# Where the first loads are issued: chunk 0 wholly on SP's queue, chunk 2 behind ScalarE's table load

## The chip, the cores and the metric

The kernel runs on one core of a Trainium2 chip. Times are microseconds (us) on the device; the profile measures one execution, and the runs are further executions. The engines are TensorE (PE, with its weight loads as PEld), VectorE (DVE), ScalarE (ACT), GpSimd (POOL) and SyncE (SP), which only issues transfers here. A queue is where an engine's transfers are issued: q1 in the profile carries those that SP issues, q10 those of ScalarE. Both are served by the core's 16 DMA engines.

## What is computed

The input x has 32 x 64 = 2048 tokens of 1024 values, all in float32.

```python
base   = einsum('btd,od->bto', x, W)                     # 1024 x 1024
logits = einsum('btd,ed->bte', x, Wr) + 5.0 * one_hot(language_ids)   # 8 experts
topw, topi = top_k(logits, 2)
gates  = sum(one_hot(topi) * softmax(topw))
h      = einsum('btd,erd->bter', x, A)                   # rank 16 for each expert
y      = base + 2.0 * einsum('bter,bte,eor->bto', h, gates, B)
out    = x + einsum('bti,oi->bto', y, (U * S) @ V.T)     # rank 256
```

## The kernel before

The last step has rank 256, so the kernel never forms y. It first makes the product of V and W, a 1024 x 256 matrix (in the code `proj`), and that of B and V (`bv`). Then it goes over 16 tiles of 128 tokens: x times `proj` (together with the columns of A and Wr), the gates, the gated rank part times `bv`, a transposition, and the product with U times S, to which x is added.

float32 products are made of float32r ones. Each operand is split into a `hi` part, a cast made by ScalarE, and a `lo` part, the rest, made by VectorE (GpSimd for x). Three multiplications (hi hi, hi lo, lo hi; the helper `triple`, lines 244 to 246) give one product. So each piece of V and W goes load, ScalarE (`v_hi` line 417, `w_hi` line 413), VectorE (`v_lo` line 492, `w_lo` line 487), TensorE.

The first phase runs over 16 chunks: V and W are cut into 8 chunks of 128 rows, and W into a left and a right half of 512 columns. Chunk k, from 0 to 7, holds 256 columns of V and the left half of W in one array `VW`, 384 KB, and has a semaphore `vw_load[k]`. The right halves (`w_raw`) come as chunks 8 to 15. TensorE makes 12 multiplications for each chunk, in order. Chunk 0 is loaded in two pieces of 192 KB: V with the first 128 columns of W, and the other 384 columns, with a semaphore `vw_rest_load`; its 12 multiplications stand in `p_first` (lines 259, 264, 269), those of the other chunks in `p_chunk`. While the first load is under way TensorE multiplies zeros (line 374).

Each engine's program is written out by hand and runs in its written order; semaphores join them. SP issues chunk 0's first piece, then chunks 1 and 3 to 7, then ids, the right halves, A, B, U and x. ScalarE issues chunk 0's second piece and chunk 2, then runs one Exp of a single column (`act_warm`), in front of which the compiled program has the load of its function table, and then the casts. The Exp reads `iota_e`, which GpSimd writes, and waits for that (`const`). After the first phase come the 16 tiles (`step`), and the stores at the end.

Of the kernel before, what the change touches and what calls it, by code (L numbers as in the profile page):

```python
# [16 lines left out]
def adaln_ffn(nc, xt, x, ids, VW, W, AW, B, U, S, out):  # L17
    P = 128
    TILES, _, DC, _ = xt.shape
    D = DC * P  # L20
    E = 8
    ER = AW.shape[2] - E
    R = ER // E
    OC, _, HQ = W.shape
    O = OC * P
    RANK = U.shape[1] * P
# [18 lines left out]
    with ExitStack() as ctx:  # L45
        def sb(name, shape, dt):
            return ctx.enter_context(nc.sbuf_tensor(name, shape, dt))
# [4 lines left out]
        def sem(name):  # L52
            return ctx.enter_context(nc.semaphore(name))
# [5 lines left out]
        vw_raw = sb("vw_raw", [P, OC, RANK + HQ], F32)  # L59
# [46 lines left out]
        vw_load = [sem(f"vw_load{k}") for k in range(OC)]  # L106
        vw_rest_load = sem("vw_rest_load")
# [52 lines left out]
        def w_chunk(i):  # L160
            return vw_raw[:, i, RANK:RANK + HQ] if i < OC else w_raw[:, i - OC, :]
# [4 lines left out]
        @block.sync  # L166
        def _(sp):
            def load_w(k):
                sp.dma_start(w_raw[:, k, :], W[k, :, :]).then_inc(w_load[k], 16)

            def load_xt(t):
                if t >= XTR:
                    sp.wait_ge(xt_lo, t - XTR + 1)
                sp.dma_start(xt_raw[:, t % XTR, :, :], xt[t, :, :, :]).then_inc(xt_load[t % XTR], 16)

            def load_x(t):
                if t >= XR:
                    sp.wait_ge(stored[t % XR], 16 * (t // XR))
                sp.dma_start(x_all[:, t % XR, :], x_v[t, :, :]).then_inc(x_load[t % XR], 16)

            def store(t):
                sp.wait_ge(fin_free, HALF * t + HALF)
                sp.dma_start(out_v[t, :, :], x_all[:, t % XR, :]).then_inc(stored[t % XR], 16)

            first = RANK + P
            sp.dma_start(vw_raw[:, 0, 0:first], VW[0, :, 0:first]).then_inc(vw_load[0], 16)
            for k in (1, *range(3, OC)):
                sp.dma_start(vw_raw[:, k, :], VW[k, :, :]).then_inc(vw_load[k], 16)
            sp.dma_start(ids_i[:, :], ids).then_inc(ids_load, 16)
            load_w(0)  # L190
            load_w(1)
            sp.dma_start(aw_raw[:, :, :], AW).then_inc(aw_load, 16)
            load_xt(0)
            load_w(2)
            load_w(3)
            sp.dma_start(b_raw[:, :, :], B).then_inc(b_load, 16)
            for k in range(4, OC):
                load_w(k)
            load_xt(1)
            sp.dma_start(s_col[:, :], S).then_inc(s_load, 16)  # L200
            sp.dma_start(u_raw[:, :, :], U).then_inc(u_load, 16)
            for t in range(2, XTR):
                load_xt(t)
            for t in range(XR):
                load_x(t)
            for s in range(TILES):
                if s + XTR < TILES:
                    load_xt(s + XTR)
                if s >= 3 and s - 3 + XR < TILES:
                    load_x(s - 3 + XR)  # L210
                if s >= 2:
                    store(s - 2)
            for n in range(HALF):
                cols = slice(n * BANK, (n + 1) * BANK)
                sp.wait_ge(fin_free, HALF * (LAST - 1) + n + 1)
                sp.dma_start(out_v[LAST - 1, :, cols], x_all[:, (LAST - 1) % XR, cols]).then_inc(stored[(LAST - 1) % XR], 16)
            for n in range(3):
                lo, hi = ((0, BANK), (BANK, BANK + BANK // 2), (BANK + BANK // 2, D))[n]
                sp.wait_ge(fin_free, HALF * LAST + n + 1)
                sp.dma_start(out_v[LAST, :, lo:hi], x_all[:, LAST % XR, lo:hi]).then_inc(stored[LAST % XR], 16)  # L220
            for j in range(XR):
                n = len(range(j, TILES, XR)) + (2 if j == LAST % XR else 1 if j == (LAST - 1) % XR else 0)
                sp.wait_ge(stored[j], 16 * n)
# [176 lines left out]
        @block.scalar  # L400
        def _(act):
            def split_w(i):
                h, k = divmod(i, OC)
                if i == 0:
                    nc.scalar.copy(w_hi[:, 0, 0:P], w_chunk(0)[:, 0:P]).then_inc(w_hi_done, 1)
                    act.wait_ge(vw_rest_load, 16)
                    nc.scalar.copy(w_hi[:, 0, P:HQ], w_chunk(0)[:, P:HQ]).then_inc(w_hi_done, 1)
                    return
                if i >= OC:
                    act.wait_ge(w_load[i - OC], 16)  # L410
                if i >= WRING:
                    act.wait_ge(w_used, i - WRING + 1)
                nc.scalar.copy(w_hi[:, i % WRING, :], w_chunk(i)).then_inc(w_hi_done, 1)

            def split_v(k):
                act.wait_ge(vw_load[k], 16)
                nc.scalar.copy(v_hi[:, k, :], vw_raw[:, k, 0:RANK]).then_inc(v_hi_done, 1)

            def split_p(b):
                act.wait_ge(w_used, OC if b < 2 else 2 * OC)  # L420
                nc.scalar.copy(proj_hi[:, 2 * b:2 * b + 2, Z0:COLS],
                               fin[b][:, :].rearrange("p (c n) -> p c n", c=2)).then_inc(p_hi, 1)

            def split_x(t):
                act.wait_ge(xt_load[t % XTR], 16 * (t // XTR + 1))
                if t >= 2:
                    act.wait_ge(pj_done, t - 1)
                nc.scalar.copy(xT_hi[:, t % 2, :, :], xt_raw[:, t % XTR, :, :]).then_inc(xt_hi, 1)  # L428

            def scale_u(m):  # L430
                nc.scalar.activation(us_hi[:, m, :], u_raw[:, m, :], ACT.Copy,  # L431
                                     scale=s_col[:, m:m + 1]).then_inc(us_hi_done, 1)

            def step(s):
                if s >= 1 and s + 1 < TILES:
                    split_x(s + 1)
                if s >= 1:
                    act.wait_ge(gt_done, s)
                    nc.scalar.copy(ghT_hi[:, :], gt[:, 0:P]).then_inc(gt_hi, 1)  # L439
                    act.wait_ge(z_done, s)  # L440
                    nc.scalar.copy(z_sb[:, :], pj[(s - 1) % 2][:, Z0:COLS]).then_inc(z_copied, 1)  # L441
                    act.wait_ge(zt_done, s)
                    nc.scalar.copy(zT_hi[:, (s - 1) % 2, :], zt[:, 0:RANK]).then_inc(zt_hi, 1)  # L443
                if s < TILES:
                    act.wait_ge(dtop_ready, s + 1)
                    nc.scalar.activation(etop[:, :], dtop[:, :], ACT.Exp, accum_out=esum[:, :]).then_inc(exp_done, 1)

            first = RANK + P
            act.dma_start(vw_raw[:, 0, first:], VW[0, :, first:]).then_inc(vw_rest_load, 16)
            act.dma_start(vw_raw[:, 2, :], VW[2, :, :]).then_inc(vw_load[2], 16)  # L450
            act.wait_ge(const, 3 + E)
            nc.scalar.activation(esum[:, :], iota_e[:, 0:1], ACT.Exp).then_inc(act_warm, 1)
            act.wait_ge(act_warm, 1)
            for i in range(2 * OC):
                if i < OC:
                    split_v(i)
                split_w(i)
                if i == OC + 1:
                    act.wait_ge(aw_load, 16)
                    nc.scalar.copy(proj_hi[:, :, 0:Z0], aw_raw[:, :, :]).then_inc(aw_hi, 1)  # L460
                if i == OC + 3:
                    split_p(0)
                    split_p(1)
                if i == OC + 4:
                    split_x(0)
                if i == OC + 6:
                    act.wait_ge(b_load, 16)
                    nc.scalar.copy(b_hi[:, :, :], b_raw[:, :, :]).then_inc(b_hi_done, 1)
            split_p(2)
            split_p(3)  # L470
            split_x(1)
            step(0)
            act.wait_ge(s_load, 16)
            act.wait_ge(u_load, 16)
            scale_u(0)
            act.wait_ge(bv_done, 1)
            nc.scalar.activation(bv_hi[:, :], bv_ps, ACT.Copy, scale=SCALING).then_inc(bv_hi_done, 1)
            scale_u(1)
            for s in range(1, TILES + 1):
                step(s)  # L480
# [186 lines left out]
```

## Time and profile before

| | |
|---|---|
| Runs before | 162.08, 162.8, 163.09 us; median 162.8 |
| The profiled execution | 161.95 us |
| Span of its profile | 160.2 us |
| TensorE busy | 154.1 us, 96% of the span |
| VectorE, ScalarE, GpSimd busy | 81.6, 55.5, 40.4 us |
| Moved by DMA | 32.69 MB, 204 GB/s over the span |

The span is that of the instructions which the profile shows; the execution's own time is 1.75 us longer. A TensorE that is busy 96% of the time is one that the others keep fed nearly everywhere.

### The profile page before, as it was taken

Reading aid. Unit: us, or ns where it says so; the run is one execution under the profiler, and the core shown is the slowest. Engines: PE = TensorE matmul, PEld = TensorE weight load, DVE = VectorE, ACT = ScalarE, POOL = GpSimd, SP = SyncE. Lnnn points to the kernel's source line nnn. Section 1 sums busy time; section 2 is a strip of 40 time slices with the busy share of each in tenths; the row PEclk is TensorE's granted clock in tenths of the full one; section 3 lists DMA queues with packets and bytes.
Section 4 is the critical chain, followed back from the end, with each engine's and each line's share of the span. In section 5 each row is a group of like instructions: output and inputs, shape, how many; then the busy total and the mean of one; then the engine's idle time right before and its main releaser. Section 6 shows DMA issues by size and latency. Waiting matters only on the chain.

```text
span 160.2 us, 2469 instructions
## 1 busy us (share of the span) xinstructions
PE 154.1 (96%) x900; PEld 142.4 (89%) x900; DVE 81.6 (51%) x260; ACT 55.5 (35%) x132; POOL 40.4 (25%) x31
## 2 busy tenths in 40 slices
PE   7599999999999999999999999999999999999992
PEld 4499999998998999999998989898989898989882
DVE  0696983455946263535444453536262717081843
ACT  4684881526334323241404041414141414111210
POOL 2000060072354150606060505142323323200000
PEclk9999999999999999999999999999999999999999
DMA  5999999973300859283837474656553430303055
GB/s 176 391 403 406 392 410 408 409 302 125 128 7 0 260 208 314 100 301 119 278 131 262 141 252 158 241 169 224 197 200 131 131 131 0 131 4 131 0 202 191
DMA packets 10522, 32.69 MB, mean 204 GB/s; under 512 B 1424, under 2 KB 1936, under 8 KB 10384
## 3 DMA queue, kind: packets, MB, share of 16 engines
q1 hardware_dynamic: 10224, 31.96, 54.5%
q10 hardware_dynamic: 288, 0.59, 1.0%
q8 instruction: 7, 0.11, 0.3%
q14 instruction: 3, 0.02, 0.1%
HBM read 24.16 MB, written 8.39 MB: 203 GB/s over the span
## 4 chain that ended last, share of the span: by engine, by line
PE 91%; DMA 3%; ACT 2%; DVE 1%; issue 0%; SPq 0%
PE pj L244 15%; PE pj L246 15%; PE pj L245 15%; PE fin L244 14%; PE fin L246 14%; PE fin L245 14%; DMA vw_raw<-in_VW 3%; PE zt L303 2%; PE gt L291 1%; ACT us_hi L431 1%; PE zt L246 1%; PE zt L244 1%; PE zt L245 1%; ACT xT_hi L428 1%; DVE w_lo L487 0%
## 5 line engine op out<-in xcount | busy, mean ns | idle before, releaser
L237 POOL TENSOR_TENSOR xT_lo<-xt_raw,xT_hi 128x1024 fp32r<-128x1024 f32 x16 | 39.3, 2454 | 95.8 <-ACT xT_hi L428 95.8
L244 PE MATMUL pj<-proj_hi,xT_hi 128*128 128x392 f32 x128 | 45.1, 352 | 0.0
L246 PE MATMUL pj<-proj_hi,xT_lo 128*128 128x392 f32 x128 | 43.6, 341 | 0.0
L245 PE MATMUL pj<-proj_lo,xT_hi 128*128 128x392 f32 x128 | 43.4, 339 | 0.0
L244 PE MATMUL fin<-us_hi,zT_hi 128*128 128x512 f32 (+1 forms) x66 | 27.0, 409 | 0.0
L246 PE MATMUL fin<-us_hi,zT_lo 128*128 128x512 f32 (+1 forms) x66 | 25.6, 388 | 0.0
L245 PE MATMUL fin<-us_lo,zT_hi 128*128 128x512 f32 (+1 forms) x66 | 25.6, 388 | 0.0
L244 PEld LDWEIGHTS pj<-proj_hi,xT_hi 128*128 128x128 f32 x128 | 24.0, 188 | 1.2
L245 PEld LDWEIGHTS pj<-proj_lo,xT_hi 128*128 128x128 f32 x128 | 24.1, 188 | 0.6
L246 PEld LDWEIGHTS pj<-proj_hi,xT_lo 128*128 128x128 f32 x128 | 24.0, 188 | 0.0
L520 DVE SCALAR_TENSOR_TENSOR logit<-target,pj 128x8 f32<-128x8 f32 x16 | 2.6, 163 | 40.6 <-PE pj L246 40.6
L565 DVE TENSOR_TENSOR x_all<-fin,x_all 128x512 f32<-128x512 f32 x31 | 21.2, 686 | 2.5 <-PE fin L246 2.5
L244 PE MATMUL fin<-v_hi,w_hi 128*128 128x256 f32 x60 | 17.1, 285 | 1.4 <-DVE w_lo L487 1.4
L245 PE MATMUL fin<-v_lo,w_hi 128*128 128x256 f32 x60 | 17.0, 283 | 0.0
L246 PE MATMUL fin<-v_hi,w_lo 128*128 128x256 f32 x60 | 17.0, 283 | 0.0
L428 ACT CAST xT_hi<-xt_raw 128x1024 fp32r<-128x1024 f32 x16 | 16.6, 1040 | 0.0
L441 ACT COPY z_sb<-pj 128x256 f32<-128x256 f32 x16 | 6.0, 374 | 25.8 <-PE pj L246 25.8
L246 PEld LDWEIGHTS fin<-us_hi,zT_lo 128*128 128x128 f32 x66 | 12.4, 188 | 2.8
L439 ACT CAST ghT_hi<-gt 128x128 fp32r<-128x128 f32 x16 | 4.3, 266 | 30.3 <-PE gt L291 30.3
L244 PEld LDWEIGHTS fin<-us_hi,zT_hi 128*128 128x128 f32 x66 | 12.4, 188 | 2.1
L245 PEld LDWEIGHTS fin<-us_lo,zT_hi 128*128 128x128 f32 x66 | 12.5, 189 | 2.0
L443 ACT CAST zT_hi<-zt 128x256 fp32r<-128x256 f32 x16 | 6.0, 374 | 22.2 <-PE zt L303 22.2
(71 smaller groups left out, 188.8 us busy)
## 6 DMA issues: line engine op xcount, KB each, us to landing
xt_raw<-in_xt SPq DMA_DIRECT2D x16, 512.0 KB, 4.1
x_all<-in_x SPq DMA_DIRECT2D x16, 512.0 KB, 3.6
out<-x_all SPq DMA_DIRECT2D x14, 512.0 KB, 2.9
vw_raw<-in_VW SPq DMA_DIRECT2D x6, 384.0 KB, 6.1
w_raw<-in_W SPq DMA_DIRECT2D x8, 256.0 KB, 9.8
u_raw<-in_U SPq DMA_DIRECT2D x1, 1024.0 KB, 13.0
out<-x_all SPq DMA_DIRECT2D x3, 256.0 KB, 2.0
aw_raw<-in_AW SPq DMA_DIRECT2D x1, 544.0 KB, 8.1
```

The costliest lines, as they stand in the source:

```text
L237: nc.gpsimd.tensor_sub(xT_lo[:, t % 2, :, :], xt_raw[:, t % XTR, :, :], xT_hi[:, t % 2, :, :].bitcast(F32)).then_inc(xt_lo, 1)
L244: nc.tensor.matmul(dst, l_hi, r_hi, start=first, stop=False, skip_group_check=shared)
L245: nc.tensor.matmul(dst, l_hi, r_lo, start=False, stop=False, skip_group_check=shared)
L246: return nc.tensor.matmul(dst, l_lo, r_hi, start=False, stop=last, skip_group_check=shared)
L291: nc.tensor.transpose(gt[:, 0:P], gh[:, :], ident[:, :]).then_inc(gt_done, 1)
L303: last = nc.tensor.transpose(zt[:, m * P:(m + 1) * P], z_sb[:, m * P:(m + 1) * P], ident[:, :])
L428: nc.scalar.copy(xT_hi[:, t % 2, :, :], xt_raw[:, t % XTR, :, :]).then_inc(xt_hi, 1)
L439: nc.scalar.copy(ghT_hi[:, :], gt[:, 0:P]).then_inc(gt_hi, 1)
L441: nc.scalar.copy(z_sb[:, :], pj[(s - 1) % 2][:, Z0:COLS]).then_inc(z_copied, 1)
L443: nc.scalar.copy(zT_hi[:, (s - 1) % 2, :], zt[:, 0:RANK]).then_inc(zt_hi, 1)
L520: nc.vector.scalar_tensor_tensor(logit[:, :], target[:, s, :], LANG_BIAS, pj[q][:, LOG:LOG + E], ALU.mult, ALU.add).then_inc(gate_step, 1)
L565: nc.vector.tensor_add(x_all[:, t % XR, cols], fin_bank(i)[:, :], x_all[:, t % XR, cols]).then_inc(fin_free, 1)
```

## The change

Chunk 0's second piece is issued by SP, between the first piece and chunk 1. ScalarE issues chunk 2 behind its Exp instead of ahead of it. Nothing else is altered; from there on line numbers differ by one or two.

```diff
             sp.dma_start(vw_raw[:, 0, 0:first], VW[0, :, 0:first]).then_inc(vw_load[0], 16)
+            sp.dma_start(vw_raw[:, 0, first:], VW[0, :, first:]).then_inc(vw_rest_load, 16)
             for k in (1, *range(3, OC)):
                 sp.dma_start(vw_raw[:, k, :], VW[k, :, :]).then_inc(vw_load[k], 16)
...
-            first = RANK + P
-            act.dma_start(vw_raw[:, 0, first:], VW[0, :, first:]).then_inc(vw_rest_load, 16)
-            act.dma_start(vw_raw[:, 2, :], VW[2, :, :]).then_inc(vw_load[2], 16)
             act.wait_ge(const, 3 + E)
             nc.scalar.activation(esum[:, :], iota_e[:, 0:1], ACT.Exp).then_inc(act_warm, 1)
+            act.dma_start(vw_raw[:, 2, :], VW[2, :, :]).then_inc(vw_load[2], 16)
             act.wait_ge(act_warm, 1)
```

ScalarE's program at its start, before. Each row is an instruction with what it writes and reads, and the semaphores that it waits for.

```order
L449 DMA vw_raw<-in_VW 128x384
L450 DMA vw_raw<-in_VW 128x768
L452 ACT_TABLE_LOAD
L452 ACTIVATE esum<-iota_e 128x1 [waits const]
L417 CAST v_hi<-vw_raw 128x256 [waits vw_load0,act_warm]
L405 CAST w_hi<-vw_raw 128x128
L407 CAST w_hi<-vw_raw 128x384 [waits vw_rest_load]
L417 CAST v_hi<-vw_raw 128x256 [waits vw_load1]
```

And ScalarE's program at its start after the change:

```order
L450 ACT_TABLE_LOAD
L450 ACTIVATE esum<-iota_e 128x1 [waits const]
L451 DMA vw_raw<-in_VW 128x768
L418 CAST v_hi<-vw_raw 128x256 [waits vw_load0,act_warm]
L406 CAST w_hi<-vw_raw 128x128
L408 CAST w_hi<-vw_raw 128x384 [waits vw_rest_load]
L418 CAST v_hi<-vw_raw 128x256 [waits vw_load1]
```

The piece of 384 columns is gone from it, and the chunk of 768 columns, chunk 2, stands behind the table load and the Exp.

SP's first instructions after the change; before, the second of these rows was not there:

```order
L186 DMA vw_raw<-in_VW 128x384
L187 DMA vw_raw<-in_VW 128x384
L189 DMA vw_raw<-in_VW 128x768 x6
L190 DMA ids_i<-in_ids 128x16
L169 DMA w_raw<-in_W 128x512 x2
```

Every load that SP issues from chunk 1 on stands one place further back.

## Rows read from the trace of the kernel before

**Rows 1.** Stretch, its us, busy us of PE, PEld, DVE, ACT, POOL; clock, DMA share, GB/s.
```profile
0.00:7.74 7.74, 4.83 (x19) 3.39 (x19) 2.29 (x5) 4.21 (x10) 1.12 (x15) 1.00 0.78 280
7.74:29.43 21.69, 21.69 (x181) 21.69 (x182) 15.47 (x25) 12.82 (x24) 2.41 (x1) 1.00 1.04 404
29.43:47.00 17.57, 17.33 (x109) 16.91 (x108) 11.62 (x31) 8.14 (x16) 7.86 (x3) 1.00 0.50 188
47.00:157.00 110.00, 110.00 (x596) 100.40 (x595) 51.82 (x200) 30.30 (x84) 29.00 (x13) 1.00 0.46 163
```

**Rows 2.** Waits of TensorE, then of ScalarE, from 0 to 30 us.
```profile
PE fin L244 <- DVE w_lo L487: 1.4, 1, 1.4
...
ACT v_hi L417 <- DMA vw_raw<-in_VW: 1.9, 2, 1.3
```

**Rows 3.** The chain that ended last, in order of time (start, us, what).
```profile
0.74 0.38 SPq L186
1.17 4.84 DMA vw_raw<-in_VW
6.03 0.41 ACT v_hi L417
6.44 0.53 ACT w_hi L413
6.99 0.70 DVE w_lo L487
7.74 0.39 PE fin L244
```

**Rows 4.** Timeline from 0 to 8 us: start, us, engine, line, operation.
```profile
0.73 0.40 ACTq L449 DMA_DIRECT2D vw_raw<-in_VW  x1
...
1.16 0.46 ACTq L450 DMA_DIRECT2D vw_raw<-in_VW  x1
1.17 2.85 SPq L188 DMA_DIRECT2D vw_raw<-in_VW  x6
...
1.55 0.33 POOL L234 MEMSET iota_e<- 128x1 f32 x8
1.65 1.28 ACT L452 ACT_TABLE_LOAD   x1 [1.65 <-PEq L657]
2.94 0.20 ACT L452 ACTIVATE esum<-iota_e 128x1 f32<-128x1 f32 x1
3.69 0.41 ACT L417 CAST v_hi<-vw_raw 128x256 fp32r<-128x256 f32 x1 [0.54 <-DMA vw_raw<-in_VW]
...
5.70 0.64 PE L269 MATMUL fin<-v_hi,w_lo 128*128 128x256 f32 x4
...
6.87 0.40 ACT L417 CAST v_hi<-vw_raw 128x256 fp32r<-128x256 f32 x1
```

**Rows 5.** DMA queues from 1 to 2.05 us: packets, MB, share of 16 engines.
```profile
q1 hardware_dynamic: 28, 0.04, 19.7%
```

**Rows 6.** DMA queues from 2.05 to 2.1 us.
```profile
q10 hardware_dynamic: 1, 0.00, 8.1%
```

**Rows 7.** DMA queues from 1 to 3.43 us.
```profile
q1 hardware_dynamic: 174, 0.29, 43.8%
q10 hardware_dynamic: 144, 0.20, 21.9%
```

**Rows 8.** DMA queues from 3.43 to 5.7 us.
```profile
DMA packets 307, 0.85 MB, mean 374 GB/s; under 512 B 31, under 2 KB 31, under 8 KB 307
q1 hardware_dynamic: 164, 0.45, 56.9%
q10 hardware_dynamic: 143, 0.39, 45.3%
```

**Rows 9.** The issue of chunk 2 on ScalarE, line 450, and its landing.
```profile
L450 ACTq DMA_DIRECT2D vw_raw<-in_VW x1: 461/461/461, 1.2 to 1.2; - x1
...
DMA to landing us min/median/max: 5.0/5.0/5.0
```

## The prediction

> **What bounds the kernel now.** The first view read is the busy time of each engine in four stretches [rows 1]. From 7.74 us on TensorE hardly pauses: it is busy 21.69 of 21.69 us, then 17.33 of 17.57 us, then all of 110.00 us, and the granted clock is 1.00 in every row. Only in the first 7.74 us is there room: 4.83 us busy. What is left behind 157 us is the last addition and the stores, which the edit does not touch. So the edit, which concerns the first microseconds alone, can move the end by as much as it moves the point at which the unbroken run of TensorE begins, and by nothing else.
>
> The second view is the list of waits [rows 2]. TensorE's one real wait there is 1.4 us at line 244, the first multiplication of chunk 1, released by VectorE's w_lo. ScalarE has two waits for a load, 1.9 us together. The third view, the chain in order of time, says what stands behind both [rows 3]: the load of chunk 1 is issued at 1.17 and lands 4.84 us later, at 6.01. ScalarE casts V from 6.03 and W up to 6.97, VectorE makes w_lo from 6.99 to 7.69, and TensorE begins chunk 1 at 7.74. From landing to TensorE it is 7.74 - 6.01 = 1.73 us, and none of that is edited.
>
> Chunk 0, whose second piece the edit moves, is not the bound. The timeline shows its last four multiplications starting at 5.70 and running 0.64 us [rows 4], so TensorE is through with it at 6.34 and idle for 1.40 us. The table load (1.65 to 2.93) and the warming Exp (to 3.14) are not the bound either: the cast that follows them starts at 3.69, at the landing of chunk 0's first piece. **Everything turns on one number, the landing of chunk 1.**
>
> **What that landing depends on.** The two queues' traffic in stretches of time tells it. Up to 2.05 us only SP's queue, q1, has moved anything [rows 5]. ScalarE's queue, q10, has its first packet in the next 0.05 us [rows 6]: 2.05 - 0.73 = 1.32 us after its first issue. By 3.43 us [rows 7] q10 has moved 0.20 MB, which is its piece of chunk 0 (192 KB, 0.197 MB) and nothing of chunk 2. q1 has moved 0.29 MB, its own 0.197 MB piece and some 0.09 MB of chunk 1. From 3.43 to 5.70 us [rows 8] q10 moves 0.39 MB, just chunk 2, while q1 moves 0.45 MB: the 0.30 MB that chunk 1 (0.393 MB) still lacked, and a part of chunk 3. The total is 374 GB/s, of which q1 gets 0.45 / 2.27 = 198 GB/s. So chunk 1 shares the DMA engines with chunk 2 for its last 0.30 MB. At that rate it would be through at 3.43 + 1.52 = 4.95; it lands at 6.01. The 1.06 us between are the slowest of 16 engines and the completion, which I take as unchanged.
>
> **Part 1, chunk 0's second piece goes to SP's queue.** The bytes that have to move ahead of chunk 1's end are the same as before: all of chunk 0, as SP's piece and the other piece ran side by side. Now the two run one behind the other, then chunk 1. At equal total rate q1 alone has moved the same 0.49 MB at 3.43 us [rows 7], and chunk 1 still lacks 0.30 MB. Cost of the bytes: 0. The issue itself takes 0.43 us on SP (its neighbours, six issues in 2.85 us, take 0.475 each with their gaps [rows 4]); it pushes chunk 1's issue from 1.17 to 1.60 and every later issue of SP by as much. q1's first packet came at 1.75 or later (no more than 0.04 MB by 2.05), about 1.0 us after its issue at 0.74, so chunk 1 is ready to move at about 2.6. By then q1 has not emptied chunk 0's 0.39 MB, which at the total rate takes until about 3.1. The 0.43 us is hidden behind those bytes; uncovered it would cost all of 0.43. The later loads of SP sit in a queue that is full anyway: 404 GB/s was moved by all engines up to 29 us, and ScalarE waits for no load there but the two named. Taken: 0.
>
> **Part 2, chunk 2's load goes behind the table load.** ScalarE's stream now starts with the table load, at about 0.73, where its first issue began. It takes 1.28 us and ends near 2.01, the last iota write is done at 1.88, and the Exp takes 0.20, to about 2.2 [rows 4]. ScalarE's issue of chunk 2 then starts between 2.02 (beside the Exp) and 2.25, and takes some 0.46 us as before [rows 9]. With 1.32 us from issue to first packet, chunk 2 starts to move between 3.34 and 3.57. Before, it started at 3.43, behind its queue mate. **The two halves of the edit nearly cancel:** chunk 2 used to be held back by a load ahead of it in the queue, and is now held back by the table load, for nearly the same time.
>
> The price of the difference: for each microsecond that chunk 2 starts later, q1 moves 374 - 198 = 176 KB more, which at 198 GB/s brings chunk 1 forward by 0.89 us. Starting at 3.34 costs 0.09 x 0.89 = 0.08 us; starting at 3.57 gains 0.14 x 0.89 = 0.12 us. I take the upper end, an issue behind the Exp, since in the trace ScalarE's issues and the table load follow one another without overlap (1.16 + 0.46 = 1.62, then 1.65): a gain of 0.1 us. Chunk 2 landed at 1.16 + 5.0 = 6.16 us [rows 9] and would at 6.3, and ScalarE reaches it at 6.87 before [rows 4], so it stays hidden. The 0.46 us of issuing on ScalarE ends by 2.7, ahead of chunk 0's cast at 3.69 or a little sooner. Chunk 0 itself may come a few tenths earlier, into the 1.40 us in which TensorE waits for chunk 1: worth nothing.
>
> **The sum.** Chunk 1 begins on TensorE at 7.74 - 0.1 = 7.64. The profiled execution took 161.95 us for a span of 160.2 us, and would take 161.85. The runs before have a median of 162.8, 0.85 above the profiled one, and lie 1.0 us apart. The same 0.1 off the median gives 162.7 us.
>
> **Rival A, chunk 1 gets the DMA engines to itself.** If chunk 2's first packet comes at or after chunk 1's last, chunk 1's missing 0.30 MB moves at 374 instead of 198 GB/s: 0.80 instead of 1.52 us, a gain of 0.7. TensorE would start chunk 1 at 7.0, still behind chunk 0's end at 6.34, so all of it counts: 162.8 - 0.7 = 162.1. It wants chunk 2's issue at 4.23 - 1.32 = 2.9 or later, 0.65 later than I have it. For it speaks that nothing in the trace shows an issue behind an Exp, and that a queue's packets may start later than the one case of 1.32; against it that the Exp took up its work 0.01 us after the table load. The Trainium skill, page "ScalarE: Activation LUTs", section "What ACT_TABLE_LOAD costs", prices a switch of tables at 1.28 us of load and about 1.38 us of drain; an estimate by it puts the issue near 3.6 and is this rival in full. By that page the time would be 162.1, while rows 4 show the load's 1.28 and no drain behind it. Chance 0.18.
>
> **Rival B, the late issue decides, and the kernel is slower.** If q1 takes up chunk 1 a fixed time after its issue and not when the ring ahead of it is empty, chunk 1 lands at 1.60 + 4.84 = 6.44 and TensorE starts it 0.43 later: 162.8 + 0.43 = 163.2. It decides from the point where chunk 1 is ready later than q1 has emptied chunk 0, 2.6 against 3.1 by my figures; the full price needs another 0.43 beyond that, or a queue that loses as much rate by running alone. For it speaks that q1 alone moved only 0.04 MB up to 2.05 us [rows 5], which the start of the engines may or may not explain, and that no row has one queue alone at the full rate before 5.7 us; against it that chunk 1's bytes followed chunk 0's on q1 before 3.43 us [rows 7] with no gap that the total shows. The Trainium skill, page "DMA: Bandwidth & Descriptors", section "Issuing engines are not separate DMA queues", speaks against the change in this way: issuing from several engines saves issue time and nothing else, and this edit gives up just that. Rows 8 agree with its other half, that the queues interleave on the same engines. Chance 0.12.
>
> **Rival C, chunk 2 comes too late.** TensorE wants chunk 2 after chunk 1's 12 multiplications (15 chunks in 21.69 us [rows 1], 1.45 each), at 9.19; with 1.73 us of casting ahead it must land by 7.46, 1.3 us later than its 6.16. That takes an issue at about 3.5. From there every microsecond of delay costs one, less the 0.7 of rival A. Only a ScalarE queue held up for over 2 us would do it. Chance 0.04, about 163.3.
>
> **How the numbers follow.** The forecast, chunk 1 within 0.2 us of its old landing, has chance 0.66 and the time 162.7. Rival A 0.18 at 162.1, rival B 0.12 at 163.2, rival C 0.04. The ends of the range are A's 162.1 less 0.3 and B's 163.2 plus 0.1, for the spread of 1.0 us between the runs themselves: 161.8 to 163.3. A measurement of this kernel can hardly tell less than 1% (1.6 us) from no change, and no rival reaches that; what is left for either side is a shift of the runs. Faster by over 1% 0.03, within 1% 0.94, slower 0.03.
>
> **What would show it.** In the changed kernel's timeline the table load starts near 0.75 and ScalarE's issue near 2.2. q10's first packet comes near 3.5, and TensorE's wait at line 245, formerly 244, grows by what chunk 0 ends sooner; chunk 1 begins between 7.5 and 7.8. Rival A shows as a start near 7.0, rival B as one near 8.1 with q1 idle before chunk 1's packets, rival C as a second gap in TensorE behind chunk 1. The forecast is wrong if a queue's rate depends on its being alone, or if the time from issue to first packet on q10 is not 1.32 us when the issue comes later.

## The result, and the profile after

The changed kernel takes 165.52 us (median of 6 runs, 164.58 to 166.88) where the kernel before takes 162.44 (6 runs, 161.83 to 163.22). The ratio is 1.0192, with a 95% interval of 1.0132 to 1.0251: 3.1 us slower. The profiled execution took 164.58 us for a span of 162.8 us, 2.6 more than the 160.2 before.

The same stretches as [rows 1], of the changed kernel, with the first 29 us cut where its clock changes:

```profile
0.00:9.90 9.90, 6.93 (x27) 5.58 (x28) 3.46 (x8) 5.37 (x13) 1.12 (x15) 1.00 0.77 276
9.90:13.30 3.40, 3.40 (x18) 3.40 (x17) 2.86 (x7) 1.76 (x5) 0.00 (x0) 0.50 1.03 397
13.30:29.00 15.70, 15.70 (x133) 15.70 (x132) 11.55 (x16) 9.98 (x16) 2.42 (x1) 1.00 1.04 404
```

From 9.90 to 13.30 us the granted clock is 0.50, 1.2 instead of 2.4 GHz. TensorE is busy all the time but starts only 18 multiplications. The same 3.40 us of the kernel before:

```profile
9.90:13.30 3.40, 3.40 (x31) 3.40 (x30) 3.10 (x7) 2.22 (x5) 0.00 (x0) 1.00 1.04 400
```

13 fewer at 0.12 us each are 1.6 us lost. The other part of the loss stands in the chain that ended last, to be set beside [rows 3]:

```profile
0.74 0.38 SPq L186
1.17 0.42 SPq L187
1.64 5.36 DMA vw_raw<-in_VW
7.03 0.40 ACT v_hi L418
7.43 0.53 ACT w_hi L414
7.99 0.70 DVE w_lo L486
8.73 0.39 PE fin L245
```

Chunk 1 is issued at 1.64 instead of 1.17, lands 5.36 us later instead of 4.84, at 7.00 instead of 6.01, and TensorE starts it at 8.73 instead of 7.74. From landing to TensorE it is 1.73 us, as before. So the profile has 1.0 us of later start and 1.6 us of half clock, 2.6 together: all of the longer span. All six executions of the changed kernel had a mean granted clock of 0.979 to 0.99 of full speed, where one such stretch in the profile makes 0.99 and the profile of the kernel before had 1.00. The two at 0.979 are 1.7 and 2.3 us above the profiled one; 0.979 would be some 6.9 us at half clock instead of 3.4, an estimate from the mean alone. The clock is not all that differs between executions: one at 0.99 is 1.4 us above the profiled one too.

What ScalarE and SP do in the first 2.1 us (timeline, beside [rows 4]):

```profile
0.73 1.28 ACT L450 ACT_TABLE_LOAD   x1 [0.73 <-PEq L656]
...
1.64 0.42 SPq L189 DMA_DIRECT2D vw_raw<-in_VW  x1
1.93 0.37 ACTq L451 DMA_DIRECT2D vw_raw<-in_VW  x1
2.03 0.20 ACT L450 ACTIVATE esum<-iota_e 128x1 f32<-128x1 f32 x1
```

ScalarE issues chunk 2 at 1.93, within the table load and ahead of the Exp that stands in front of it in the program. The issue waited for the iota writes (1.88), not for the table.

The queues' traffic up to 3.43 us and from there to 5.7 us, as in [rows 7] and [rows 8]:

```profile
DMA packets 293, 0.41 MB, mean 168 GB/s; under 512 B 32, under 2 KB 288, under 8 KB 293
q1 hardware_dynamic: 291, 0.40, 55.5%
q10 hardware_dynamic: 2, 0.01, 2.8%
...
DMA packets 207, 0.63 MB, mean 277 GB/s; under 512 B 2, under 2 KB 2, under 8 KB 207
q1 hardware_dynamic: 106, 0.32, 46.6%
q10 hardware_dynamic: 101, 0.31, 36.4%
```

q1 has moved 0.40 MB by 3.43, chunk 0's 0.393 and hardly anything of chunk 1, where before the two queues had moved 0.49. Then the two queues together reach 277 GB/s instead of 374. Split by the microsecond, the hole stands where chunk 0's bytes end:

```profile
2.00:3.00 1.00, 1.00 (x4) 0.79 (x3) 0.00 (x0) 0.22 (x2) 0.00 (x0) 1.00 0.81 295
3.00:4.00 1.00, 0.92 (x3) 0.20 (x2) 0.28 (x1) 0.72 (x3) 0.00 (x0) 1.00 0.57 134
4.00:5.00 1.00, 0.97 (x4) 0.94 (x5) 0.82 (x2) 0.29 (x1) 0.00 (x0) 1.00 0.86 289
5.00:6.00 1.00, 1.00 (x6) 1.00 (x6) 0.02 (x1) 0.00 (x0) 0.00 (x0) 1.00 1.02 396
```

134 GB/s from 3 to 4 us, where the kernel before has 349:

```profile
3.00:4.00 1.00, 0.92 (x3) 0.20 (x1) 0.00 (x0) 0.46 (x2) 0.00 (x0) 1.00 0.98 349
```

The DMA engines had nothing to do, or waited. The question for the experiments is why.

### The profile page after: what moved, and what is told of

It reads as the page before. It is cut to its first block, busy times and chain, and to the rows that moved or that the text cites. A ratio compares the mean times of both kernels' runs of the same rounds, so it can differ in the third digit from the quotient of the medians.

```text
span 162.8 us, 2469 instructions
## 1 busy us (share of the span) xinstructions
PE 156.5 (96%) x900; PEld 144.9 (89%) x900; DVE 81.8 (50%) x260; ACT 55.6 (34%) x132; POOL 40.4 (25%) x31
## 4 chain that ended last, share of the span: by engine, by line
PE 91%; DMA 3%; ACT 2%; DVE 1%; SPq 0%; issue 0%
PE pj L245 15%; PE pj L247 15%; PE pj L246 15%; PE fin L245 14%; PE fin L247 14%; PE fin L246 14%; DMA vw_raw<-in_VW 3%; PE zt L304 2%; PE gt L292 1%; ACT us_hi L432 1%; PE zt L247 1%; PE zt L245 1%; PE zt L246 1%; ACT xT_hi L429 1%; DVE w_lo L486 0%
## 5 line engine op out<-in xcount | busy, mean ns | idle before, releaser
L245 PE MATMUL fin<-v_hi,w_hi 128*128 128x256 f32 x60 | 17.8, 297 | 1.9 <-DVE w_lo L486 1.9
L247 PE MATMUL fin<-v_hi,w_lo 128*128 128x256 f32 x60 | 17.7, 295 | 0.0
L246 PE MATMUL fin<-v_lo,w_hi 128*128 128x256 f32 x60 | 17.6, 294 | 0.0
L245 PEld LDWEIGHTS fin<-v_hi,w_hi 128*128 128x128 f32 x60 | 12.2, 204 | 2.1 <-DVE w_lo L486 2.1
```

Of the source, the lines that this page charges most:

```text
L245: nc.tensor.matmul(dst, l_hi, r_hi, start=first, stop=False, skip_group_check=shared)
L246: nc.tensor.matmul(dst, l_hi, r_lo, start=False, stop=False, skip_group_check=shared)
L247: return nc.tensor.matmul(dst, l_lo, r_hi, start=False, stop=last, skip_group_check=shared)
```

## The experiments

Times are medians. Each ratio is to runs of the kernel before on the same chip, with its 95% interval. "Lands" is issue plus time to landing, from the profile of that kernel, which is one execution. Unedited loads show how far one profile can be trusted: chunk 1 lands at 6.0 us in the kernel before, at 5.6 in e4 and at 5.4 in e14, which have the same loads, and at 7.0 in the changed kernel and 7.5 in e3, which share theirs. So the change made chunk 1 later by something between 1.0 and 2.1 us, and where the loads are shared by both queues, a difference of half a microsecond between two profiles says little. The runs are called e1 to e16; each diff is against the kernel that the text or the expectation names.

### Each half of the change alone

e1: chunk 0's second piece to SP, chunk 2 left at the head of ScalarE's program:

```diff
 sp.dma_start(vw_raw[:, 0, 0:first], ...).then_inc(vw_load[0], 16)
+sp.dma_start(vw_raw[:, 0, first:], ...).then_inc(vw_rest_load, 16)
-act.dma_start(vw_raw[:, 0, first:], ...).then_inc(vw_rest_load, 16)
```

> Only the first half of the change: chunk 0's second piece on SP's queue, chunk 2 still issued by ScalarE ahead of its table load. In the changed kernel the DMA engines moved only 134 GB/s from 3 to 4 us and chunk 1 landed at 7.0 instead of 6.0 us. Theory S (supply): chunk 1 is now the third transfer on q1, and its packets are not there when q1 has emptied chunk 0, whatever q10 does. Then chunk 1's packets on q1 again begin at 3.1 us or later for most engines, and it lands at 6.4 us or later. Rival H (the fresh queue): the gap comes from chunk 2, which as the first transfer of its queue starts at 3.2 to 4.4 us and holds the engines up. Then chunk 2 moves from 2.1 us on, there is no gap, and chunk 1 lands at 6.0 us or before. In time: S +0.5 to +1.0 us against the kernel before from the load alone, H 0. A stretch of TensorE at half clock would add up to 1.7 us.

162.99 us, ratio 1.0025 (0.9999 to 1.0052). Chunk 1, issued at 1.65, lands 4.6 us later, at 6.3. By landing this is near S. By traffic the hole of 3 to 4 us is gone (378 and 409 GB/s from 3 to 5 us), as H has it, but another one stands a microsecond earlier:

```profile
2.00:3.00 1.00, 1.00 (x4) 0.79 (x3) 0.00 (x0) 0.65 (x2) 0.00 (x0) 1.00 0.53 134
```

Here it is chunk 0 that comes late: its first piece lands 3.8 us after its issue instead of 2.9, ScalarE casts it at 4.63 instead of 3.69, and TensorE then never waits for chunk 1. Neither theory is right as it stands.

e2: chunk 2 behind the Exp, chunk 0's second piece left where it was:

```diff
-act.dma_start(vw_raw[:, 2, :], VW[2, :, :]).then_inc(vw_load[2], 16)
 act.wait_ge(const, 3 + E)
 nc.scalar.activation(esum[:, :], iota_e[:, 0:1], ACT.Exp).then_inc(act_warm, 1)
+act.dma_start(vw_raw[:, 2, :], VW[2, :, :]).then_inc(vw_load[2], 16)
```

> Only the second half of the change: chunk 2 issued by ScalarE behind table load and Exp, chunk 0's second piece still on q10 ahead of it. Theory S: chunk 1 is the second transfer on q1 as before, so it starts behind its own piece of chunk 0 and lands at 6.0 us or earlier, down to 5.3 us if chunk 2 comes late enough to leave it the engines; time 0 to -0.7 us. Rival H: chunk 2's late start holds the engines up, chunk 1 lands near 7.0 us and the time is +1.0 us or more.

163.78 us, ratio 1.0076 (1.0044 to 1.0108). Chunk 1 lands after 3.6 us, at 4.8: with less on q10 beside it, it is earlier than in any profile with the loads of before. H falls. But chunk 2, issued at 1.93, takes 6.6 us and lands at 8.56, 2.4 later than before, and the rate is 246 to 304 GB/s from 4 to 7 us. TensorE waits for it, and starts it at 10.28:

```profile
10.28 0.39 PE L244 MATMUL fin<-v_hi,w_hi 128*128 128x256 f32 x1 [0.45 <-DVE w_lo L487]
```

The kernel before starts chunk 2 at 9.19. The difference, 1.1 us, is that of the two spans (161.3 and 160.2). So the second half loses by itself, 1.1 us by the medians; the first half costs 0.3 us, at the edge of its interval. Together they cost 3.1, more than the sum of both.

### TensorE's clock

e3 and e4: the changed kernel, and the kernel before, with multiplications of zeros between chunks 0 and 1 (8 and 6 of them):

```diff
 p_first()
+for _ in range(8):
+    nc.tensor.matmul(gt[...], zeros[:, :], zero_row, start=True, stop=True)
```

> The changed kernel with 8 more multiplications of zeros (512 columns, into a bank not yet in use) between chunk 0 and chunk 1, where TensorE stood idle for 1.87 us ahead of a stretch at half clock (9.90 to 13.31 us). Theory C (clock): the idle time brings the half clock about; filled, the granted clock stays at 1.00 from the first rise to the end, and 1.7 us come back, so the time is 1.0 to 1.7 us below the changed kernel's 165.5. Rival: the clock falls by itself, and the low stretch of 3.4 us appears as before; the time is the changed kernel's or more, since the added multiplications may delay chunk 1.

164.3 us, ratio 1.0093 (1.0061 to 1.0125), 1.2 us below the changed kernel (1.6 by the two ratios). The same stretch as above:

```profile
9.90:13.30 3.40, 3.40 (x30) 3.40 (x30) 3.40 (x9) 3.08 (x8) 0.00 (x0) 1.00 1.04 402
```

No half clock, and 30 multiplications, although chunk 1 landed even later here, at 1.64 + 5.89 = 7.5. Nine of its ten executions have a mean clock of 0.998 or more; one has 0.989, at 166.2 us. Theory C holds for these nine: without the idle time ahead of chunk 1 the half clock stays away. No length of idle time at which the clock falls can be read from the runs. The kernel before idles for 1.40 us there without a fall, the changed one for 1.87 with one.

> The kernel before with 6 more multiplications of zeros between chunk 0 and chunk 1, where it idles for 1.40 us. Its profile has no stretch at half clock behind the first rise, so theory C expects no change of the profiled time beyond 0.3 us; if some of its executions do have such a stretch (they spread over 1.4 us), the median falls by up to 0.7 us and the spread narrows. Rival: the additions only delay chunk 1, +0.2 to +0.5 us.

162.71 us, ratio 1.0002 (0.9963 to 1.0041). The median says no change, but no execution lies near it: six take 161.9 to 162.1 us, six 163.3 to 164.5. For the first six C is right. The profile is one of the others, and there the rival is: the six additions start at 7.34, run at half pace until 9.4 us, and hold chunk 1 back to 9.67, though its w_lo was ready at 7.3. Half pace shows in the number of multiplications started in a microsecond, from 5 to 6 us, first in the kernel before, then in e4:

```profile
5.00:6.00 1.00, 1.00 (x10) 1.00 (x10) 0.43 (x1) 0.00 (x0) 0.00 (x0) 1.00 1.00 369
5.00:6.00 1.00, 1.00 (x6) 1.00 (x6) 0.50 (x1) 0.39 (x2) 0.00 (x0) 1.00 1.03 412
```

In e4 the multiplications of chunk 0 stand 0.21 us apart, and the full pace of 0.12 us comes at 9.4 us; in the profile of the kernel before it came before chunk 0's second four. The clock column says 1.00 in both, since it knows no level ahead of the first change. TensorE's first microseconds run at half pace, and for how long differs from one profile to the next.

e14 and e15: two kernels that take the idle time away at the start, where TensorE has nothing to do between its 6 multiplications of zeros and chunk 0:

```diff
-for n in range(6):
+for n in range(7):
     nc.tensor.matmul(fin[n % FINS][...], zeros[:, :], zero_row, start=True, stop=True)
```

This is e14; e15 has `range(8)` on top of e9's edit, below.

> The kernel before with 7 multiplications of zeros at the start instead of 6, which cover 0.43 of the 0.52 us that TensorE idles ahead of chunk 0. In the profiles TensorE comes up from half clock between 4.3 and 15.4 us, and the runs of one kernel spread over 1.5 us and more. Theory C (clock: idle time at the start delays the rise): the median falls by 0.2 to 0.8 us below 162.6 and the spread narrows. Rival: the rise does not depend on the idle time; the median stays within 0.2 us.

**161.93 us, ratio 0.9966 (0.9941 to 0.9990).** The only kernel of the sixteen that is clearly faster than the one before, by 0.55 us by the ratio, within the range that C gave. Nine of its 12 runs lie between 161.75 and 162.26; those of the kernel before beside it are spread from 161.76 to 163.44. The gain is measured. That it comes from an earlier full pace is argued: its one profile has the full pace from 6.1 us on, later than the profile of the kernel before, and its span of 159.8 also has a chunk 1 that landed at 5.4.

> All loads on SP with chunk 0 as one transfer (median 162.58, TensorE idle for 0.83 us ahead of chunk 0 and not at all ahead of chunk 1), with 8 multiplications of zeros at the start instead of 6, which last to about 4.77 us, where chunk 0 starts. TensorE then runs without a pause from 0.99 us on. Theory C: the rise comes before 7.8 us in the profile and the median falls to 161.6 to 162.3, below the kernel before. Rival: no change, 162.6 within 0.2.

162.27 us, ratio 0.9987 (0.9962 to 1.0013), with the full pace from 3.9 us on in the profile. In the expected direction and inside the range, but not apart from the kernel before.

### All on SP, or chunk 2 on SP

e5: the kernel before with chunk 2 on SP.

```diff
-for k in (1, *range(3, OC)):
+for k in range(1, OC):
     sp.dma_start(vw_raw[:, k, :], VW[k, :, :]).then_inc(vw_load[k], 16)
...
-act.dma_start(vw_raw[:, 2, :], VW[2, :, :]).then_inc(vw_load[2], 16)
```

> The kernel before with chunk 2 issued by SP between chunks 1 and 3, so that q10 carries only chunk 0's second piece, at 0.73 us. In the run with only chunk 2 moved, chunk 1 landed at 4.83 us while q10 was silent, and the slow stretch (246 to 304 GB/s from 4 to 7 us, chunk 2 landing at 8.56) came with the late issue of chunk 2. Theory L (late issue): the issue at 1.93 us on ScalarE's queue, into traffic under way, brings the slow stretch. Without it the rate stays near 400 GB/s, chunk 1 lands at 4.9 and chunk 2 at 5.9 us; TensorE has no idle time but at the start, and the time is 0.3 to 1.0 us below the kernel before. Rival T (third transfer): the third transfer on q1 is slow by itself, wherever chunk 2 is; then the stretch from 4 us on is there again, chunk 2 lands at 6.5 us or later and the time is at or above that of the kernel before.

162.60 us, ratio 0.9996 (0.9978 to 1.0014). Chunk 1 lands after 3.6 us, at 4.8, and TensorE never waits for it. The landing of chunk 1:

```profile
DMA to landing us min/median/max: 3.6/3.6/3.6
```

But the slow stretch is there without any late issue on ScalarE: chunk 2, issued at 1.6, lands at 6.9. Theory L falls as stated, T holds by the profile. The time moved by nothing; in this profile chunk 0's work at half pace lasted until 7.4 us, so that the early landing could not be used.

e6: the same edit made to the changed kernel, so that ScalarE issues nothing.

> The changed kernel with chunk 2 issued by SP between chunks 1 and 3: ScalarE issues nothing. Theory L: no slow stretch, chunk 1 lands at 4.8 to 5.1 us behind both pieces of chunk 0, chunk 2 at 5.9, time 0 to 0.8 us below the kernel before. Rival T: the third transfer on q1, chunk 1, again starts late (over 200 KB missing in 3 to 4 us as in the changed kernel) and lands near 6.5 to 7 us; time +1 to +3.

162.82 us, ratio 1.0025 (0.9997 to 1.0052). Chunk 1, issued at 1.65, lands after 4.8 us, at 6.4: T's landing, but not its time. With no late chunk 2 beside it, chunk 1 comes 0.6 us before the changed kernel's. The hole from 3 to 4 us is the same, though q10 carries nothing at all:

```profile
3.00:4.00 1.00, 0.92 (x4) 0.23 (x2) 0.32 (x1) 0.76 (x3) 0.00 (x0) 1.00 1.05 134
```

So the late chunk 2 does not make the hole. The twelve executions also price the clock within one kernel: three have a mean clock of 0.988 or 0.989 and a median of 164.3 us, the other nine have 0.997 or more and a median of 162.8.

e9: e6 with chunk 0 as one transfer.

```diff
-sp.dma_start(vw_raw[:, 0, 0:first], VW[0, :, 0:first]).then_inc(vw_load[0], 16)
-sp.dma_start(vw_raw[:, 0, first:], VW[0, :, first:]).then_inc(vw_rest_load, 16)
+sp.dma_start(vw_raw[:, 0, :], VW[0, :, :]).then_inc(vw_load[0], 16)
...
-act.wait_ge(vw_rest_load, 16)
```

> All loads on SP as in the run with all of them there, but chunk 0 as one transfer of 384 KB: chunk 1 is the second transfer on q1 and not the third, with the same bytes ahead of it. So far the third transfer on q1 landed between 6.3 and 7.7 us in every kernel, the second at 3.7 to 4.8 or, sharing with q10, at 5.6 to 6.0. Theory P (place in the queue): chunk 1 lands at 4.8 to 5.1 us, and chunk 2, now the third, at 6.3 to 7.5; TensorE has no wait ahead of chunk 1 above 0.5 us; time 162.3 to 162.8. Rival Y (bytes and moment): the rate falls near 3.3 us because q1 runs alone, and chunk 1 again lands at 6.3 us or later; time 162.8 to 165.

162.58 us, ratio 1.0003 (0.9972 to 1.0035). Chunk 1 second and issued at 1.17: it lands after 3.7 us, at 4.9. Chunk 2 is late instead, at 6.5. One issue fewer ahead of chunk 1, the same bytes, and 1.5 us gained on its landing. Y falls. One more thing differs from e6, and no run separates it: chunk 0 as one transfer goes in packets of 2 KB and more (111 of them from 1 to 3 us), as two pieces in smaller ones (254).

e10: chunk 1 instead of chunk 2 on ScalarE, at the head of its program.

```diff
-for k in (1, *range(3, OC)):
+for k in range(2, OC):
...
+act.dma_start(vw_raw[:, 1, :], VW[1, :, :]).then_inc(vw_load[1], 16)
 act.wait_ge(const, 3 + E)
```

> Both pieces of chunk 0 on SP, chunk 1 issued by ScalarE at 0.73 us ahead of the table load, chunk 2 by SP as the third transfer on q1. Theory P: chunk 1 shares the engines with chunk 0 and lands at 4.4 to 5.0 us, chunk 0 at 4.2 to 4.6, chunk 2 as the third at 6.3 to 7.0; the third's lateness is covered by TensorE's work on chunks 0 and 1, time 162.3 to 162.9. Rival Y: q10's early traffic keeps the rate up, so that chunk 2 lands at 5.9 us or before; the time is the same within the noise.

162.88 us, ratio 1.0026 (0.9997 to 1.0055). Chunk 1 lands at 4.3, chunk 2, issued at 1.6 on SP, at 7.1. P holds, a little beyond its ranges.

### Where ScalarE's issue stands

e7: the issue ahead of the Exp and its table load, but behind the wait.

```diff
 act.wait_ge(const, 3 + E)
+act.dma_start(vw_raw[:, 2, :], VW[2, :, :]).then_inc(vw_load[2], 16)
 nc.scalar.activation(esum[:, :], iota_e[:, 0:1], ACT.Exp).then_inc(act_warm, 1)
-act.dma_start(vw_raw[:, 2, :], VW[2, :, :]).then_inc(vw_load[2], 16)
```

> The changed kernel with chunk 2's issue at the same time, behind the wait for the iota writes (1.88 us), but ahead of the table load, which then runs from about 2.3 us. In the changed kernel the issue stood at 1.93, inside the table load. Theory L: the same slow stretch, chunk 1 lands at 6.5 to 7.5 us, time near the changed kernel's 165.5. Rival B (table load): the issue is slow in its effect because it runs during the table load; without that chunk 1 lands at 5.5 to 6.0 us and the time is that of the kernel before, 162.6 within 0.5.

165.64 us, ratio 1.0168 (1.0129 to 1.0206), chunk 1 at 1.64 + 6.06 = 7.7. It is not the place within the table load that makes the issue harmful: at the same moment, 1.92, it does the same harm ahead of the load. But the time is lost in another way than in the changed kernel. All six executions have a mean clock of 0.998 or more, and in the profile the half pace of the start lasts until 15.4 us, under a column of 1.00:

```profile
10.00:11.00 1.00, 1.00 (x7) 1.00 (x6) 1.00 (x3) 1.00 (x3) 0.00 (x0) 1.00 1.05 398
```

The kernel before starts 11 multiplications in that microsecond.

e8: the issue behind the casts of chunk 0.

```diff
 split_w(i)
+if i == 0:
+    act.dma_start(vw_raw[:, 2, :], VW[2, :, :]).then_inc(vw_load[2], 16)
```

> The changed kernel with chunk 2's issue another 2 us later, behind ScalarE's casts of chunk 0 (near 3.9 us). Theory L: the slow stretch moves with the issue, so chunk 1 (landed by then or nearly) comes at 4.8 to 5.3 us and chunk 2 late, at 8 us or later, so that TensorE's gap stands ahead of chunk 2; time +1 to +3. Rival T: the stretch stays at 3.3 us and chunk 1 lands near 7 us. If the rate stays near 400 GB/s throughout, both are wrong, and what matters is that the issue at 1.93 meets the first packets.

166.68 us, ratio 1.0223 (1.0184 to 1.0261). The profile is of the longest of the six executions, 168.9 us, with half clock from 8.9 to 19.2 us. Chunk 1 lands at 6.7, so it is not spared. Chunk 2, issued at 3.73, takes 7.7 us and lands at 11.4; TensorE waits twice, 4.1 us together. L is right on chunk 2 and wrong on chunk 1, T the other way about.

### Place or moment

In all kernels so far the late transfer on q1 was both the third and issued at 1.6. e11 is e5 with a small load (ids, 8 KB) in the second place:

```diff
 sp.dma_start(vw_raw[:, 0, 0:first], ...).then_inc(vw_load[0], 16)
+sp.dma_start(ids_i[:, :], ids).then_inc(ids_load, 16)
 for k in range(1, OC):
```

> The kernel with chunk 2 on SP (chunk 1 landed at 4.8 us there, second on q1), with the small load of ids (8 KB) moved from behind the chunks to the second place, so that chunk 1 is the third transfer and its issue is 0.45 us later, while 8 KB more lie ahead of it. Theory P: chunk 1 lands at 6.3 us or later. Rival Y: it lands at 4.8 to 5.2 us.

163.19 us, ratio 1.0025 (0.9994 to 1.0057). Chunk 1 lands after 4.1 us, at 5.75: between the two, later than Y by 0.5 and earlier than P by as much. e13 is e5 with chunk 1 kept in its second place, but issued at 1.64:

```diff
 sp.dma_start(vw_raw[:, 0, 0:first], ...).then_inc(vw_load[0], 16)
+sp.wait_ge(const, 3)
 for k in range(1, OC):
```

> The kernel with chunk 2 on SP (chunk 1 second on q1, issued at 1.17, landing at 4.8 us), where SP waits behind its first issue for GpSimd's identity (done at 1.61), so that chunk 1 keeps its second place but is issued at about 1.65, as it is in the changed kernel. The same bytes lie ahead of it. Theory P (place: the third transfer on a queue is late): chunk 1 lands at 4.8 to 5.3 us. Theory M (moment: what is issued once the traffic is about to run, from 1.6 us on, is late, and the third transfer was late because its issue came at 1.6): chunk 1 lands at 5.7 us or later, as in the run with ids in the second place (5.75). Time: P 162.3 to 162.9, M 162.6 to 163.5.

162.91 us, ratio 1.0016 (0.9991 to 1.0041). Chunk 1 takes 4.1 us again and lands at 5.8. Its issue at line 189, its time to landing:

```profile
DMA to landing us min/median/max: 4.1/4.1/4.1
```

P falls, M holds: the same second place, the same bytes ahead, 0.47 us later issued, 1.0 us later landed. Here the profiles agree with one another: 3.6 or 3.7 us in e2, e5, e9 and e15, all issued at 1.17, and 4.1 in e11 and e13. The times of e5 and e13 do not tell the two apart. In e16 the whole group of first issues is shifted, with the distances kept:

```diff
+sp.wait_ge(const, 3)
 sp.dma_start(vw_raw[:, 0, 0:first], ...).then_inc(vw_load[0], 16)
...
+act.wait_ge(const, 3)
 act.dma_start(vw_raw[:, 0, first:], ...).then_inc(vw_rest_load, 16)
```

> The kernel with chunk 2 on SP, where both engines hold back their first issue until GpSimd's identity is done at 1.61 us, so that the first packets come 0.9 us later and chunk 1 is issued at about 2.1, in the same distance from them as at 1.17. Theory M1 (an issue is late in its effect when it comes close to or behind the first packets): chunk 1, issued 0.45 us behind the first issue, lands 3.6 us after its issue, at 5.7 to 5.9. Rival M2 (the time since the program's start counts, or what other engines do then): chunk 1 lands 4.1 us or more after its issue, at 6.2 or later. The time is 0.5 to 1.5 us above the kernel before in both.

163.49 us, ratio 1.0042 (1.0018 to 1.0066). Chunk 1 is issued at 2.07 and takes 3.6 us:

```profile
DMA to landing us min/median/max: 3.6/3.6/3.6
```

So it isn't the time since the start that counts, but the distance behind the first issue: 0.43 us behind it a transfer of 384 KB landed after 3.6 us, 0.9 us behind it after 4.1. That is not the whole rule: in e6 chunk 1 is also issued 0.9 us behind the first, with q10 silent, and takes 4.8. What is different there is that both pieces of chunk 0 lie ahead of it on its own queue.

e12: the changed kernel, SP holding its later loads back.

```diff
 for k in (1, *range(3, OC)):
+    if k == 3:
+        sp.wait_ge(vw_load[1], 16)
     sp.dma_start(vw_raw[:, k, :], VW[k, :, :]).then_inc(vw_load[k], 16)
```

> The changed kernel, where SP waits for chunk 1's landing before it issues chunks 3 to 7 and the rest. Theory G (one generator for both queues, worked off in the order of issue): chunk 1 is as late as in the changed kernel, 6.5 to 7.5 us, since what stands ahead of it is the same. Rival K (crowding): the later issues, at 0.45 us each, slow down the packets of the earlier ones; without them chunk 1 lands at 4.8 to 5.5 us and chunk 2's first packet comes 1.3 us after its issue at 1.93. In both cases chunk 3 comes late, so that the time is above the changed kernel's 165.5 or near it.

165.75 us, ratio 1.0212 (1.0174 to 1.0249), chunk 1 at 1.64 + 5.9 = 7.5. K falls: with the later loads held back, only chunks 1 and 2 are in flight behind the end of chunk 0, and still they move slowly:

```profile
2.00:3.00 1.00, 1.00 (x4) 0.79 (x3) 0.00 (x0) 0.22 (x2) 0.00 (x0) 1.00 0.92 315
3.00:4.00 1.00, 0.92 (x3) 0.22 (x2) 0.30 (x1) 0.74 (x3) 0.00 (x0) 1.00 1.23 121
4.00:5.00 1.00, 0.99 (x4) 0.94 (x5) 0.81 (x2) 0.28 (x1) 0.00 (x0) 1.00 0.49 120
```

From 3 to 4 us the DMA engines count as busy (1.23) while they move 121 GB/s: a packet takes long without moving more. G's landing came true, but G itself, one generator that works the issues off in their order, does not fit the kernel before, where four transfers were issued by 1.17 and all moved at 374 GB/s.

## Why the prediction was wrong

The bound was read rightly. All that the edit did to the load side went through chunk 1's landing, from there it was 1.73 us to TensorE in both profiles, and the sums of the prediction hold as sums. Chunk 0 came sooner (cast at 3.28 instead of 3.69), to no use, as forecast.

**The step that failed is part 1**, "The 0.43 us is hidden behind those bytes". I took 1.0 us from issue to first packet for chunk 1 because the first issue had it, and so had it ready at 2.6, ahead of the end of chunk 0 at 3.1. It was not ready: q1 moved hardly a byte of it by 3.43. An issue 0.9 us behind the first one is served later than by its 0.47 us of delay. With chunk 2 out of the way that costs 1.0 us (4.8 against 5.8 in e13), with all of chunk 0 ahead on the same queue 1.6 (6.4 in e6). What holds the packets up is open. Alone, with chunk 2 issued early, this half cost only 0.3 us of time (e1), and in its profile TensorE lost that time to a late chunk 0 and a long half pace, not to a wait for chunk 1. Rival B named this mechanism, and the sign, with 0.12. Its price was a constant 4.84 from issue to landing, 0.43 us, and it was 1.0.

**Part 2 failed too, and alone it cost more: 1.1 us (e2).** The issue came at 1.93, earlier than my 2.02 to 2.25: it does not stand behind the table load, and e7 shows that its place within the load does not matter. That was a few tenths. The Trainium skill, page "ScalarE: Activation LUTs", section "What ACT_TABLE_LOAD costs", prices a drain of 1.38 us with a switch of tables; here none held anything up, by the Exp's 2.03 behind a load that ends at 2.01. What I did not see is that the time from issue to landing isn't fixed. On q10 it was 4.1 us for an issue at 0.73 (e1), 4.6 to 5.0 at 1.16 (e14, e4, before), 5.3 to 6.6 at 1.93 (after, e2), 7.7 at 3.73 (e8). "The two halves of the edit nearly cancel" compared starts, and the trace of before had no issue later than 1.16 on that queue. Rival C gave chunk 2 until 7.46 us to land and asked for an issue near 3.5 to miss it; in e2 an issue at 1.93 landed at 8.56, and C's wait is what bounded that kernel. The late chunk 2 then also slows chunk 1, 6.4 without it (e6) and 7.0 to 7.7 with it (after, e3, e7, e12).

**A whole term was missing.** "the granted clock is 1.00 in every row" was taken as given for the changed kernel too. For the first row it was not even a reading: the column has no level ahead of its first change, and e4 and e7 show long starts at half pace under a column of 1.00. Chunk 1 started 1.0 us later, with 1.87 us of idle time ahead of it instead of 1.40, and a stretch at half clock came with it, 1.6 us of the profiled 2.6, more in the executions with a mean clock of 0.979; the filled kernel got 1.2 of it back. In the profiled execution the price of a wait ahead of TensorE was taken as its length, and was more than twice that. The rule that the edit moves the end by as much as the start of the unbroken run, "and by nothing else", is the sentence that fell.

The range ended at 163.3. B's mechanism at its measured size alone gives 162.4 + 1.0 = 163.4, with the clock's 1.6 it is 165.0. The median was 165.5; the executions at 0.979 can make up the rest, but none of them was profiled.

## What to carry to other kernels

The first transfers of a program are not to be priced by a constant time from issue to landing: one more issue or wait of 0.45 us ahead of the critical load delayed its landing by 1.0 to 1.5 us here (e13 against e5, e6 against e9), and the time by much less, wherever TensorE had no use for the early landing. So the load that gates the compute engine belongs among the first issues of whichever queue is free, and a small piece in front of it delays it (e11: 8 KB, 0.9 us). Price a new wait of TensorE by its length plus the clock that it may cost, here 1.6 us on top of a start that was 1 us later in the changed kernel, and 1.5 us in three executions of twelve in e6. And where TensorE has nothing to do at the start, a multiplication of zeros that ends just as the first data comes is worth trying: one more of them gave the only version that measured faster than both kernels, 161.93 us. Behind the first data such additions can also do harm, as in half of the executions of e4.

## What the runs showed of the hardware that was not expected

- An issue on ScalarE's queue goes out ahead of an Exp that stands before it in the program, and within the table load (1.93 against 2.03 and 0.73 to 2.01). In e2 it is 0.5 us ahead of the Exp (1.93 against 2.46), in e8 ahead of a cast (3.73 against 3.86). In all kernels that wait for the iota writes ahead of it, it came 0.04 or 0.05 us behind their end at 1.88.
- 384 KB on SP's queue, second in place: 3.6 us from issue to landing when issued 0.43 us behind the first transfer, at 1.17 (e2, e5) and at 2.07 (e16) alike, and 4.1 us when issued 0.9 us behind it (e13).
- DMA engines can count as busy at a third of their rate: 1.23 of their time for 121 GB/s from 3 to 4 us in e12, 404 GB/s at 1.04 later. What the packets wait for is open. It isn't the number of transfers in flight (e12), nor the issue's place within the table load (e7), nor a late chunk 2 (e6), nor the place in the queue alone (e13), nor the time since the start (e16).
- The clock column says nothing of the time ahead of its first change: in e4 and e5 the multiplications ran at 0.21 us apart until 9.4 and 10.3 us under a column of 1.00, in e14 until 6.1, in e15 until 3.9, in e7 until 15.4. This half pace may make a good part of the spread of 1.7 us between executions of one kernel, but so may the landings, which differ by 0.6 us between profiles with the same loads. Neither share was measured.
